# Graph network with two normalised layers: who copies the planes, who interleaves them back, and where the row statistics stand

## The reference, cut to what matters

```
agg = segment_sum(x[src], dst);  h = (1 + eps) * x + agg
h = relu(batch_norm(h @ W1 + b1));  h = relu(batch_norm(h @ W2 + b2))
x = layernorm(x + (x + h))                       # rows of 512
h = relu(x @ V1 + c1) @ V2 + c2                  # V1: 512 x 256, V2: 256 x 512
x = layernorm(x + h + segment_sum(h[src], dst))
```

## Time and profile before

| | |
|---|---|
| median of 3 runs | 254.96 us |
| the profiled execution | 255.28 us, of it span 253.1 us |
| busy: PE, DVE, ACT, POOL | 231.9, 159.3, 134.0, 84.5 us |
| share of the chain that ended last: PE, DVE, DMA, ACT | 66%, 14%, 7%, 7% |
| mean granted TensorE clock | 0.97 |

### The profile page before, as it was taken

One profiled execution on the slowest core, in us unless ns is written; L12 is line 12 of the kernel. 1 busy time (PEld: TensorE's weight loads), 2 busy tenths in 40 slices (PEclk: granted clock), 3 DMA queues, 4 the chain that ended last, 5 costly groups with the idle time before them and its releaser, 6 DMA issues.

```text
span 253.1 us, 3841 instructions
## 1 busy us (share of the span) xinstructions
PE 231.9 (92%) x1433; PEld 199.4 (79%) x1433; DVE 159.3 (63%) x369; ACT 134.0 (53%) x226; POOL 84.5 (33%) x75
## 2 busy tenths in 40 slices
PE   0837999999999999999999999999999699999991
PEld 0826998777888888888888888888889698888970
DVE  1769799873966343455555237361789989685374
ACT  0726674654867067454555406353735537935473
POOL 5510000003920006565655400404096449501241
PEclk9975999999999999999999999999999889999998
DMA  4378600000066501111000195505049900000334
GB/s 107 143 228 223 165 3 0 4 0 5 0 261 245 181 0 44 41 41 41 3 0 0 29 213 104 104 3 104 1 78 162 209 0 0 3 0 0 128 123 157
DMA packets 32323, 19.96 MB, mean 79 GB/s; under 512 B 21928, under 2 KB 27085, under 8 KB 32303
## 3 DMA queue, kind: packets, MB, share of 16 engines
q1 hardware_dynamic: 31796, 19.45, 29.2%
q0 software_dynamic: 160, 0.13, 0.2%
q10 hardware_dynamic: 346, 0.10, 0.2%
HBM read 8.51 MB, written 5.92 MB: 57 GB/s over the span
## 4 chain that ended last, share of the span: by engine, by line
PE 66%; DVE 14%; DMA 7%; ACT 7%; issue 2%; SPq 1%; POOL 1%; DVEq 0%
PE ps L1249 22%; PE ps L1193 17%; PE ps L1312 9%; PE ps L1330 6%; PE ps L1266 5%; PE ps L1279 4%; DMA plane_T<-planes 3%; DVE xT L964 2%; DVE hot_s L817 2%; PE ps L1173 2%; ACT xr L678 2%; DMA src_i<-in_src 2%; DMA pairs<-pair 2%; ACT planes L669 1%; DVE small_t L919 1%
## 5 line engine op out<-in xcount | busy, mean ns | idle before, releaser
L919 DVE BATCH_NORM_STATS2 small_t<-ps 128x6 f32<-128x500 f32 (+1 forms) x36 | 21.6, 600 | 41.4 <-PE ps L1249 25.2
L1193 PE MATMUL ps<-AT,xh 128*128 128x500 f32 (+2 forms) x120 | 43.2, 370 | 0.0
L1193 PE MATMUL ps<-AT,xl 128*128 128x500 f32 (+2 forms) x120 | 41.4, 355 | 0.0
L1249 PE MATMUL ps<-h0h,wh 128*128 128x500 f32 (+1 forms) x96 | 33.9, 353 | 0.0
L1249 PE MATMUL ps<-h0h,wl 128*128 128x500 f32 (+1 forms) x96 | 33.9, 353 | 0.0
L1249 PE MATMUL ps<-h0l,wh 128*128 128x500 f32 (+1 forms) x96 | 33.8, 352 | 0.0
L470 POOL TENSOR_TENSOR wl<-w1s,wh 128x512 fp32r<-128x512 f32 x8 | 10.1, 1302 | 47.2 <-ACT AT L544 47.2
L475 POOL TENSOR_TENSOR wl<-w2s,wh 128x512 fp32r<-128x512 f32 x8 | 11.1, 1384 | 43.9 <-ACT wh L646 43.9
L1193 PEld LDWEIGHTS ps<-AT,xh 128*128 128x128 f32 (+1 forms) x120 | 23.1, 192 | 2.7
L1193 PEld LDWEIGHTS ps<-AT,xl 128*128 128x128 f32 (+1 forms) x120 | 23.1, 192 | 2.7
L544 ACT ACTIVATE AT<-ps 128x500 fp32r<-128x500 f32 x25 | 14.7, 590 | 18.4 <-PE ps L1173 18.1
(11 more groups left out here) (144 smaller groups left out, 497.7 us busy)
## 6 DMA issues: line engine op xcount, KB each, us to landing
turns<-half_out SPq DMA_DIRECT2D x10, 320.0 KB, 2.2
out<-x SPq DMA_DIRECT2D x9, 256.0 KB
w1s<-in_L_gnn_W SPq DMA_DIRECT2D x4, 512.0 KB, 6.0
w2s<-in_L_gnn_W SPq DMA_DIRECT2D x8, 256.0 KB, 2.8
xs<-in_x SPq DMA_DIRECT2D x1, 1280.0 KB, 7.8
xs<-in_x SPq DMA_DIRECT2D x1, 1024.0 KB
lws<-in_L_gnn_W SPq DMA_DIRECT2D x1, 512.0 KB, 4.9
lw2s<-in_L_gnn_W SPq DMA_DIRECT2D x1, 512.0 KB, 4.2
```

Source lines behind the costliest of these rows:

```text
L919: link(nc.vector.bn_stats(stats[:, 6 * c:6 * c + 6], ps[:, zbank(t, c), 0:c1 - c0]))
L1193: last = mm(o, part[0:r, k, d * P:d * P + P], AT[0:r, k, c0:c1], start=(k == 0 and j == 0), stop=(k == NT - 1 and j == 1))
L1249: last = mm(ps[:, zbank(t, c), 0:c1 - c0], w[:, t, d * P:d * P + P], h[c][:, d, :], start=(d == 0 and j == 0), stop=(d == DT - 1 and j == 2))
```

## The change

Both planes are copied by ACT (`to_planes`), so DVE loses `plane_high`. Interleaving is shared: ACT takes node tiles 0 to 4 and POOL 5 to 9 (`XR_SPLIT` = 5), two copies of 640 elements each instead of two of 1280. ACT's share of block 2 moves behind the root of the last block; POOL's stands between `widen(4)` and `widen(5)`. `lw1_low` moves from d = 2 to d = 1. The row statistics of part 0 all stand behind the third sum, `xp_sum(2)`, ahead of `xp_low_mid`; those of part 1 for tiles 0 to 4 ahead of the last sum, for 5 to 9 behind `ln_stats(0)`. `widen(6)` and `widen(7)` wait for the last block of `xpl`, 8 and 9 move one place back. On PE `hidden_early(6)` to `(8)` move ahead of a set of transposes.

```diff
 SP:     for d in range(DT - 1):
-            sp.wait_ge(plane_lo, d + 1)
-            sp.wait_ge(plane_hi, d + 1)
             if d >= 1:
-                sp.wait_ge(xr_set, 2 * d)
+                sp.wait_ge(xr_act, 2 * d)
+                sp.wait_ge(xr_pool, 2 * d)
+            sp.wait_ge(plane_set, 2 * d + 2)
 POOL:
+        def rows_back(d):
+            pl.wait_ge(planes_T, 32 * (d + 1))
+            if d < DT - 2:
+                pl.wait_ge(xph_set, d + 1)
+                pl.wait_ge(xpl_set, d + 1)
+            else:
+                pl.wait_ge(xpl_mid, 1)
+            for i in range(2):
+                nc.gpsimd.tensor_copy(xr_half(d, XR_SPLIT, NT, i), plane_T[i][:, XR_SPLIT:NT, :].rearrange(
+                    "p k c -> p (k c)")).then_inc(xr_pool, 1)
         for d in range(DT - 2):
             xp_low(d)
+            rows_back(d)
-        for k in range(NT - 2):
+        for k in range(5):
             widen(k)
+        rows_back(DT - 2)
+        widen(5)
         pl.wait_ge(xpl_last, 2)
-        widen(NT - 2)
+        widen(6)
+        widen(7)
         for j, k in enumerate(UL_POOL):
             u_low(k, j)
-            if j == 0:
-                widen(NT - 1)
+            if j in (1, 2):
+                widen(7 + j)
 ACT, affine(t), behind the root:
+            if t == BT - 1:
+                rows_back(DT - 2)
 ACT:    for d in range(DT):
             affine(HT + d)
             if d < DT - 1:
-                plane_low(d)
+                to_planes(d)          # both halves, two copies of 1250
             xp_high(d)
-            if d < DT - 1:
-                rows_back(d)
             if d == 1:
                 ...                   # lw1h
+            if d < DT - 2:
+                rows_back(d)          # node tiles 0 to 4 only
 DVE, batch_norm(t), between the mean and the reciprocal:
-            if t == BT - 1:
-                for k in range(2):
-                    row_stats(k, 1)
 DVE:    for d in range(DT):
             batch_norm(HT + d)
-            if d == DT - 2:
-                for k in range(4):
-                    row_stats(k, 0)
             if d == DT - 1:
-                for k in range(2, 7):
+                for k in range(XR_SPLIT):
                     row_stats(k, 1)
             xp_sum(d)
-            if d < DT - 1:
-                v.wait_ge(xp_set, d + 1)
-                plane_high(d)
             if d == 0:
                 lw1_sum()
             if d == 1:
                 lw1_center()
+                lw1_low()
             if d == 2:
+                for k in range(NT):
+                    row_stats(k, 0)
                 xp_low_mid(d)
-                lw1_low()
-                for k in range(4, NT):
-                    row_stats(k, 0)
-        for k in range(7, NT):
-            row_stats(k, 1)
         ...
         xp_low_last(0)                # now waits for xr_act and xr_pool too
         xp_low_last(1)
         ln_stats(0)
+        for k in range(XR_SPLIT, NT):
+            row_stats(k, 1)
         ln_stats(1)
 PE:
+        hidden_early(6)
         xp_rows(0)
-        hidden_early(6)
         hidden_last(0)
+        hidden_early(7)
         xp_rows(1)
-        hidden_early(7)
         hidden_last(1)
+        hidden_early(8)
         xp_rows(2)
-        hidden_early(8)
         hidden_last(2)
```

More of the change, by code:

```diff
@@ L252, in gnn_kernel @@
         xp_set, xph_set, xpl_set, xpl_last = (sem(n) for n in ("xp_set", "xph_set", "xpl_set", "xpl_last"))
+        pads_set = sem("pads_set")
         rows_T, ln_var, ln_std_s, ln_aff, x1_last_set, x1_set = (
             sem(n) for n in ("rows_T", "ln_var", "ln_std_s", "ln_aff", "x1_last_set", "x1_set"))
-        plane_lo, plane_hi, planes_T, xr_set, row_part, xpl_mid = (
-            sem(n) for n in ("plane_lo", "plane_hi", "planes_T", "xr_set", "row_part", "xpl_mid"))
+        plane_set, planes_T, xr_act, xr_pool, row_part, xpl_mid = (
+            sem(n) for n in ("plane_set", "planes_T", "xr_act", "xr_pool", "row_part", "xpl_mid"))
         u_sum, u32_set, uh_set, ur_set, ul_pool, ul_dve = (
@@ L286, in gnn_kernel, with xr_half @@
         assert RT == 4 and NT == 10 and sorted(sum(LN_SETS, [])) == list(range(NT))
+        XR_SPLIT = NT // 2
         def half_of(a, i):
             return a.bitcast(I16).rearrange("p (n i) -> p n i", i=2)[:, :, i]
+        def xr_half(d, k0, k1, i):
+            return half_of(xr[:, d, k0:k1, :].rearrange("p k c -> p (k c)"), i)
         def row_at(k):
@@ L618, in _, with rows_back @@
                 act.wait_ge(spilled[i], 16 * cdiv(NT - i, ATS))
+            def rows_back(d):
+                act.wait_ge(planes_T, 32 * (d + 1))
+                act.wait_ge(xph_set, d + 1)
+                if d < DT - 2:
+                    act.wait_ge(xpl_set, d + 1)
+                else:
+                    act.wait_ge(xpl_mid, 1)
+                for i in range(2):
+                    nc.scalar.activation(xr_half(d, 0, XR_SPLIT, i), plane_T[i][:, 0:XR_SPLIT, :].rearrange(
+                        "p k c -> p (k c)"), ACT.Copy).then_inc(xr_act, 1)
             def affine(t):
@@ L663, in xp_high, with to_planes @@
                     nc.scalar.activation(xph[:, d, c0:c1], xT[:, d, c0:c1], ACT.Copy).then_inc(xph_set, 1)
-            def plane_low(d):
+            def to_planes(d):
                 act.wait_ge(xp_set, d + 1)
@@ L668, in plane_low @@
                     act.wait_ge(planes_T, 32 * d)
[L669 to L674, removed]
                 else:
-                    act.wait_ge(xpl_mid, 1)
+                    act.wait_ge(pads_set, 1)
                 for i in range(2):
-                    nc.scalar.activation(half_of(xr[:, d, :, :].rearrange("p k c -> p (k c)"), i),
-                                         plane_T[i][:, :, :].rearrange("p k c -> p (k c)"), ACT.Copy).then_inc(xr_set, 1)
+                    nc.scalar.activation(plane[i][:, 0:N], half_of(xT[:, d, :], i), ACT.Copy).then_inc(plane_set, 1)
             for d in range(DT):
@@ L899, in row_stats @@
                 r = rows[k]
-                v.wait_ge(xr_set, 4 + 2 * part)
+                v.wait_ge(*((xr_act if k < XR_SPLIT else xr_pool), 4 + 2 * part))
                 src = xr[0:r, 0:2, k, :] if part == 0 else xr[0:r, 2, k, :]
                 nc.vector.bn_stats(ln_s[0:r, k, 6 * part:6 * part + 6], src).then_inc(row_part, 1)
[L904 to L909, removed]
             def batch_norm(t):
@@ L985, in xp_low_mid @@
                                         ALU.subtract).then_inc(xpl_mid, 1)
+            v.wait_ge(z_sum, HT)
+            nc.vector.memset(planes[:, 2 * N:N + NT * P], 0).then_inc(pads_set, 1)
             for d in range(DT):
                 batch_norm(HT + d)
-                if d == DT - 2:
-                    for k in range(4):
-                        row_stats(k, 0)
                 if d == DT - 1:
-                    for k in range(2, 7):
+                    for k in range(XR_SPLIT):
                         row_stats(k, 1)
                 xp_sum(d)
-                if d < DT - 1:
-                    v.wait_ge(xp_set, d + 1)
-                    plane_high(d)
                 if d == 0:
@@ L1013, in xp_low_last @@
                 v.wait_ge(xph_set, DT + j)
+                v.wait_ge(xr_act, 2 * (DT - 1))
+                v.wait_ge(xr_pool, 2 * (DT - 1))
                 nc.vector.tensor_tensor(xpl[:, DT - 1, c0:c1], xT[:, DT - 1, c0:c1], xph[:, DT - 1, c0:c1].bitcast(F32),
@@ L1019, in ln_stats @@
                 v.wait_ge(rows_T, bank_rows(ks[-1]))
-                v.wait_ge(row_part, 2 * NT)
+                v.wait_ge(row_part, NT + XR_SPLIT if ks[-1] < XR_SPLIT else 2 * NT)
                 for k in ks:
```

## The result

The changed kernel takes 253.03 us (median of 5 runs, 252.52 to 253.34), the kernel before beside it 254.86 (254.27 to 254.99): a ratio of 0.9927, 95% interval 0.9905 to 0.995, so 1.8 us less by the medians (1.3 to 2.4 by the interval). The forecast was 252.6 (range 251.8 to 253.5), 2.4 us less; so the time lies in the range, with three quarters of the gain. The profiled execution took 252.69 with a span of 250.7, against 255.28 and 253.1.

A forecast was written before the change was run, and what follows sets the result against it. PE was taken as the bound, losing time to a late last sum and slowed clock. Terms 0.2 + 2.0 + 1.2 and more, partly given back at tiles 0 to 4, made 2.4 us: 252.6 on the median, range 251.8 to 253.5.

The forecast's parts named there:

- DVE's list ahead of the last batch norm: DVE before the last block's batch statistics: these start at 190.7 instead of 192.67, 1.97 us earlier.
- From there to PE at `neighbours`: Last batch statistics to PE's `neighbours`: first `u_scale` at 203.55, 2.47 earlier; PE there at 206.2, 4.2 earlier.
- The sum's first part freed from POOL: Last sum on DVE: its 750 part takes 0.9 us instead of 1.87, with `widen(6)` and `(7)` held back.
- POOL's copies: POOL's two interleaving copies of 640 elements: 1.4 us the pair, hidden for d = 0 and 1.
- Rival (c): POOL's strided copies for d = 2: over 5.4 us they delay `xp_low_last`, from about 8 the change is slower; chance 0.07.
- The next wait: PE ahead of tile 4 of `neighbours`: stands 1.5 us for POOL's low part, passing at 211.55, 2.4 us earlier.
- the closing sum: Whole kernel: 0.2 + 2.0 + 1.2 and more, with the copies' cost, given partly back at tiles 0 to 4: 2.4 us.
- 1.2 and more for the clock: PE in the last block: without a long idle time its clock stays at 2.4 GHz, worth 1.2 us and more.
- The remainder at d = 1: The weight's remainder on DVE, 2.2 us at its last place: costs nothing while DVE has a free stretch.
- Rival (b): PE behind 206 us: its clock falls again after waits, losing 1.7 us; gain 0.7, time 254.2; chance 0.14.
- (a): PE at `neighbours`: POOL's low parts come in time, PE alone is the bound; gain 4.2 or less, 250.8; chance 0.14.

The follow-up runs named there:

- stats_back: The changed kernel with the weight's remainder and six row statistics of part 0 back behind `xp_low_mid`, four ahead of the third sum: 255.25 us, ratio 1.0017.
- stats_alone: The kernel before with only the remainder one block forward, six statistics ahead of `xp_low_mid`, and ACT's weight high part ahead of interleaving: 252.91 us, ratio 0.9935.
- widen_early: The changed kernel with `widen(6)` and `widen(7)` no longer waiting for the last `xpl`, so beside the last sum: 254.69 us, ratio 0.9998.
- alone_low: stats_alone with POOL's `widen(9)` behind all four of its low parts: 252.7 us, ratio 0.9918 to the kernel before.
- alone_hold: alone_low with `widen(6)` and `widen(7)` held behind the last `xpl`, interleaving still on ACT alone: 252.03 us, ratio 0.9903 to the kernel before.
- low_first: The changed kernel with `widen(8)` and `widen(9)` behind all four low parts of POOL instead of between them: 251.47 us, ratio 0.9854 to the kernel before.
- act_all: The changed kernel with all interleaving on ACT, two copies of 1280 per block, none on POOL: 256.1 us, ratio 1.0046 to the kernel before.

## Why the prediction was right

- *DVE's list ahead of the last batch norm* was the cause, and 2.0 us its size: with PE's end as zero, the statistics start at 0 instead of 2.0; stats_back loses everything and stats_alone, with the ACT copy that it needs, has everything. What the remainder and the statistics bring each for itself was not run. DVE had 1.87 us to spare, not the 0.9 of the prediction: the third sum, "left where it was", starts 8.4 ahead of PE's end instead of 7.8, since ACT no longer comes late to block 2's root, ahead of which it had copied the weight's high part.
- *From there to PE at `neighbours`* the steps came out as summed, counted from PE's end: ReLU 3.95 us behind it (predicted 194.7 - 190.7 = 4.0), last sum 5.2 (5.3), first `u_scale` 12.7 (12.85), `neighbours` 15.7 (15.7).
- *The sum's first part freed from POOL*: 0.9 forecast in place of 1.87; it took 0.94, and both parts now take 1.53. widen_early prices the hold: without it the change would have brought nothing.
- *POOL's copies*: 1.74 the pair, not 1.4; hidden as said, `widen(5)` behind them still waited for its DMA. Rival (c) needed 5.4. The 2.8 that the prediction worked out from the Trainium skill's page "GPSIMD Engine Reference" (Elementwise — side-by-side cycle accounting) did not come either: the page puts its 2.6 cycles down to two inputs, and this copy has one.
- *The next wait*: POOL's low part of tile 4, 1.49 us (predicted 1.5). Counted from PE's end it came 0.3 later than summed, mostly because `widen(8)` and the second operation took 1.43 and 1.25 instead of 1.23 and 0.93 (DVE's own low parts ran beside them; that these are the reason was not tested). So the change brought 2.1 us in the profiled execution, not 2.4; that its time came out at the forecast, 252.69 against 252.9, is luck, because this execution also reached the last block 0.4 sooner.
- *Wrong in the closing sum*: it counted "1.2 and more for the clock" as a term. The rows of before forbid that: tile 4 was ready from POOL at 213.72 and used at 213.94, so a PE without slow clock would have stood there instead. Two executions of the kernel before, beside stats_back and alone_low, bear this out: their mean granted clock was 0.997 and 0.998, though a stretch like the earlier trace rows alone takes 0.007 from the mean, so the clock can't have fallen like that in them; they took 254.44 and 254.37 us, only 0.2 and 0.4 under the medians beside them. The gain was set by how much earlier POOL's low parts started, 2.6 us counted from PE's end (204.03 - 190.26 against 207.05 - 190.70), less 0.7 by which POOL took longer to the end of tile 4's (7.33 instead of 6.67), plus 0.2 that this had lain ready for PE before. One `widen` stands ahead of tile 4 in both kernels, `widen(9)` before and `widen(8)` after.
- *Not foreseen*: that the sharing, ACT's plane copies and PE's order would bring nothing measurable to this time. They shorten PE's way by 0.5 us (alone_hold against low_first), which POOL's list took back, and without the sharing the plane copies on ACT made the kernel slower than before (act_all).
- *The remainder at d = 1* took 3.08 us beside POOL's `xp_low`, not 2.2, and began only at 173.59, 3.4 us into DVE's free stretch, since it waits for the weight's high part from ACT, which the prediction left out. It ended at 176.6, just as block 2's statistics were due. That it cost nothing is luck; act_all shows what it costs when it comes 2 us later.
- Rival (b) did not come: the clock stayed at 1.00 behind a wait of 1.49 us. Nor did (a): PE stood for that wait.

## What to carry to other kernels

Count the gain at the place where two chains meet: a shorter chain gains only up to the slack of the other, and what stands in the other's list ahead of that place (here one cast ahead of POOL's low part of tile 4, 1.65 us by low_first) comes off it. When a change has several parts, run the cheapest alone; here moving a few instructions on DVE's list, and one copy on ACT's, was all of the gain. And keep POOL off a two-input VectorE operation that stands on the path: in widen_early that was worth as much as the whole change.

## What the runs showed of the hardware

- POOL's casts beside VectorE: two-input operations of 750 and 500 elements went from 1.53 to 2.5 and 2.6 us the pair (widen_early), while ten one-input statistics took 3.36 us beside POOL's `widen`, 0.34 each, as they did without it (1.40 for four in stats_back). DVE's 16-bit plane copy took 0.81 us where it began ahead of POOL's cast, while that cast and the next took 2.85 together (stats_alone; 2.42 in the changed kernel, without the copy), and 1.72 where it began behind one (kernel before).
- A 16-bit POOL copy that writes every other 16-bit word took 0.87 us for 640 elements, 1.4 ns each, against 0.98 for the cast of the earlier trace rows.
- PE's waits of 1.4 to 1.8 us in one piece (changed kernel, stats_alone, alone_low, widen_early) left the granted clock at 1.00 behind them; the wait of 2.2 us in the kernel before was followed by the 0.66 of the earlier trace rows. These are single profiles, and in two executions of the kernel before the clock can't have fallen so (mean 0.997 and 0.998); what decides between the two stays open.
